# An attention and expert layer on one core: low-part subtractions and result sums all on VectorE, ScalarE's steps two slots behind

## The reference

```python
xn = layernorm(x)
s = attention(xn)          # layernorm, q = xn @ Wq (8 heads of 64), one shared k and v, l2-normed q and k,
                           # softmax(q k^T) v, @ Wout, layernorm
y = experts(xn)            # top 2 of 8 experts with a capacity, gelu MLP 256 -> 1024 -> 256, gated sum
return x + s * silu(y)
```

## Time and profile before

| | |
|---|---|
| median of 3 runs | 3028.18 us (3024.03 to 3028.85) |
| profiled execution | 3029.31 us, its span 3027.6 us |
| TensorE busy | 2777.8 us, 92% |
| VectorE busy | 2012.2 us, 66% |
| ScalarE busy | 1910.8 us, 63% |
| GpSimd busy | 1125.2 us, 37% |
| mean granted TensorE clock | 0.974 of full speed |
| low parts on VectorE, L1194 | 817 instructions, 1347 ns mean |
| low parts on GpSimd, L1313 | 215 instructions, 2049 ns mean |
| sums of the result on GpSimd, L1306 | 64 instructions, 1263 ns mean |
| exponentials, L843 | 1032 instructions, 1015 ns mean |

### The profile page before, as it was taken

How to read it: one execution, slowest core, us unless ns; L and a number is a source line. 1 busy time by engine, 2 the same in 40 slices (tenths; PEclk the granted TensorE clock), 3 DMA queues, 4 the chain that set the end, 5 groups by cost and what they waited for, 6 DMA issues and landing times.

```text
span 3027.6 us, 86214 instructions
## 1 busy us (share of the span) xinstructions
PE 2777.8 (92%) x38213; PEld 1847.3 (61%) x38277; DVE 2012.2 (66%) x2798; ACT 1910.8 (63%) x2435; POOL 1125.2 (37%) x707
## 2 busy tenths in 40 slices
PE   4999999988999989999999999999888889888896
PEld 3566666655666657666666666655555555555564
DVE  5777787789888733333333343378788888888775
ACT  6777767756766655565656565466666666666664
POOL 2444444414787400000000000055566656566454
PEclk8999999999999989999999999999999999999997
DMA  2213222003332011221121221101111111111101
GB/s 98 93 66 109 89 76 92 28 32 99 126 120 85 6 55 50 79 72 65 63 86 59 68 74 51 38 24 32 49 47 42 49 42 40 42 43 44 30 23 45
DMA packets 111013, 184.12 MB, mean 61 GB/s; under 512 B 12648, under 2 KB 78128, under 8 KB 110640
## 3 DMA queue, kind: packets, MB, share of 16 engines
q1 hardware_dynamic: 98352, 145.04, 14.6%
q0 software_dynamic: 12288, 33.57, 3.5%
HBM read 92.58 MB, written 85.98 MB: 59 GB/s over the span
## 4 chain that ended last, share of the span: by engine, by line
PE 64%; DVE 17%; ACT 9%; issue 7%; POOL 2%; DMA 1%; SPq 0%; ACTq 0%; DVEq 0%; POOLq 0%
PE pair L607 15%; PE bank L687 14%; PE pair L673 14%; DVE arena L1194 9%; ACT arena L843 6%; PE bank L637 5%; PE bank L628 4%; PE bank L626 4%; PE bank L588 2%; PE bank L546 2%; DVE o_rest L1129 1%; PE bank L657 1%; DVE q_n L1115 1%; POOL routed_rows L1271 1%; PE bank L576 1%
## 5 line engine op out<-in xcount | busy, mean ns | idle before, releaser
L1194 DVE TENSOR_TENSOR arena<-arena 128x1024 bf16<-128x1024 f32 (+1 forms) x817 | 1091.9, 1347 | 351.6 <-ACT arena L843 349.0
L843 ACT ACTIVATE arena<-pair 128x1024 f32<-128x1024 f32 (+1 forms) x1032 | 1017.2, 1015 | 319.4 <-PE pair L607 309.7
L607 PE MATMUL pair<-qT,kT 128*128 128x512 f16 (+1 forms) x4096 | 903.0, 388 | 136.7 <-ACT arena L843 133.6
L626 PE MATMUL bank<-vhl,arena 128*128 128x65 bf16 x8192 | 654.4, 194 | 4.0 <-DVE att L1187 4.0
L1313 POOL TENSOR_TENSOR arena<-arena 128x1024 bf16<-128x1024 f32 (+1 forms) x215 | 440.6, 2049 | 578.6 <-ACT arena L843 561.3
L628 PE MATMUL bank<-vhl,arena 128*128 128x64 bf16 x8192 | 655.0, 195 | 0.0
L626 PEld LDWEIGHTS bank<-vhl,arena 128*128 128x128 bf16 x8192 | 573.6, 100 | 56.3 <-DVE att L1187 4.4
L628 PEld LDWEIGHTS bank<-vhl,arena 128*128 128x128 bf16 x8192 | 555.3, 98 | 52.3 <-issue 1.9
L607 PEld LDWEIGHTS pair<-qT,kT 128*128 128x128 f16 (+1 forms) x4096 | 205.5, 96 | 598.8 <-issue 405.0
L1243 POOL TENSOR_TENSOR q_small<-q_small,minus_half 128x8 f32<-128x8 f32 x64 | 142.8, 2231 | 1015.8 <-DVE q_small L1111 1014.8
L637 PE MATMUL bank<-vhl,arena 128*128 128x65 bf16 x8192 | 421.2, 194 | 22.9 <-DVE arena L1194 17.1
(11 more groups left out here) (191 smaller groups left out, 2448.6 us busy)
## 6 DMA issues: line engine op xcount, KB each, us to landing
routed_rows<-h_f SPq DMA_DIRECT2D x80, 256.0 KB, 4.5
att<-routed_rows SPq DMA_DIRECT2D x40, 512.0 KB, 4.3
expert_rows<-att SPq DMA_DIRECT2D x40, 512.0 KB, 2.9
raw<-in_L_ffn_w SPq DMA_DIRECT2D x32, 512.0 KB
xn_rows<-s_hl SPq DMA_DIRECT2D x16, 512.0 KB, 2.9
xT_out<-xn_rows SPq DMA_DIRECT2D x64, 128.0 KB
w_lo<-in_L_attn_x SPq DMA_DIRECT2D x64, 128.0 KB
out<-w_lo SPq DMA_DIRECT2D x64, 128.0 KB, 2.0
```

The costliest lines, as they stand in the source:

```text
L607: t = nc.tensor.matmul(into, kT[g // BG % 2][rows, part, keys], qT[g % 2][rows, h, :], start=(turn == 0), stop=(turn == 1))
L626: nc.tensor.matmul(bank[:, at:at + DH + 1], p_top[:, s, cols, 1], V[:, kb, 0:DH + 1], start=(kb == 0 and qb == 0), stop=False, skip_group_ ...
L843: nc.scalar.activation(p_f32[:, n % NP, columns(n)], pairs[n % 2][:, columns(n)], ACT.Exp).then_inc(exped, 1)
L1194: nc.vector.tensor_tensor(p_lo[:, n % NP, c], p_f32[:, n % NP, c], p_top[:, n % NP, c, 1], ALU.subtract).then_inc(lowed, 1)
```

## The change

The set `on_pool` and its semaphore go: VectorE makes the low part of every step. The sum with x in `combine` is made on VectorE, right behind the product, instead of on GpSimd. ScalarE's cast of q and VectorE's low part of q stand one and two slots later (7 and 9) for all but the first four tiles; in `combine` f_both moves to slot 10, the tanh to 12, silu, product and sum to 14, the store to 16. No amount of work changes.

```diff
-    on_pool = [n % 4 == 3 and not R_AT <= place["scores", n] < SCATTER_AT + 2 * NT for n in range(NSTEP)]
-    pool_to = np.cumsum(on_pool).tolist()
...
-                pe.wait_ge(lowed, n + 1 - pool_to[n])
-                pe.wait_ge(lowed_pool, pool_to[n])
+                pe.wait_ge(lowed, n + 1)
...
-                yield from clock.at(Q_AT[t_id] + 6)
+                yield from clock.at(Q_AT[t_id] + (6 if t_id < GT else 7))
                 act.wait_ge(q_scaled, t_id + 1)
...
-                yield from clock.at(C_AT[t_id] + 10)
+                yield from clock.at(C_AT[t_id] + 12)
                 act.wait_ge(f_both, i + 1)
...
-                yield from clock.at(Q_AT[t_id] + 7)
+                yield from clock.at(Q_AT[t_id] + (7 if t_id < GT else 9))
                 dve.wait_ge(q_hi, t_id + 1)
...
-                yield from clock.at(C_AT[t_id] + 9)
+                yield from clock.at(C_AT[t_id] + 10)
                 dve.wait_ge(f_first, i + 1)
...
-                yield from clock.at(C_AT[t_id] + 12)
+                yield from clock.at(C_AT[t_id] + 14)
                 dve.wait_ge(c_tanh, i + 1)
...
+                dve.wait_ge(c_times, i + 1)
+                dve.wait_ge(x_again_loaded[i % 2], 16 * (i // 2 + 1))
+                dve.wait_ge(out_stored[i % 2], 16 * (i // 2))
+                nc.vector.tensor_tensor(res[i % 2], w, x_again[i % 2], ALU.add).then_inc(c_added, 1)
...
-                    if a is not None and not on_pool[a]:
+                    if a is not None:
                         low(a)
...
-                yield from clock.at(C_AT[t_id] + 14)
-                pool.wait_ge(c_times, i + 1)
-                pool.wait_ge(x_again_loaded[i % 2], 16 * (i // 2 + 1))
-                pool.wait_ge(out_stored[i % 2], 16 * (i // 2))
-                nc.gpsimd.tensor_tensor(res[i % 2], c_work[i % 2][:, D:2 * D], x_again[i % 2],
-                                        ALU.add).then_inc(c_added, 1)
...
-                yield from clock.at(C_AT[t_id] + 15)
+                yield from clock.at(C_AT[t_id] + 16)
                 sp.wait_ge(c_added, i + 1)
```

More of the change, by code:

```diff
@@ L361, in build_program @@
                              "q_hi", "q_lo", "q_turned", "qT_copied")]
-        scored, exped, lowed, lowed_pool, weighed = [sem(n) for n in (
-            "scored", "exped", "lowed", "lowed_pool", "weighed")]
+        scored, exped, lowed, weighed = [sem(n) for n in ("scored", "exped", "lowed", "weighed")]
         head_inv, divided = sem("head_inv"), sem("divided")
@@ L1301, in combine @@
                         bass.IndirectOffsetOnAxis(gather_from[k][:, t_id:t_id + 1], 0)).then_inc(y_gathered[i % 2], 16)
-                yield from clock.at(C_AT[t_id] + 14)
-                pool.wait_ge(c_times, i + 1)
-                pool.wait_ge(x_again_loaded[i % 2], 16 * (i // 2 + 1))
-                pool.wait_ge(out_stored[i % 2], 16 * (i // 2))
-                nc.gpsimd.tensor_tensor(res[i % 2], c_work[i % 2][:, D:2 * D], x_again[i % 2],
-                                        ALU.add).then_inc(c_added, 1)
[L1309 to L1314, removed]
             def main(kind, a, b):
-                if kind == "att" and a is not None and on_pool[a]:
-                    low(a)
+                pass
             clock.run(slots, main, [constants()] + [statistics(g) for g in reversed(range(NG))] + [route()] + [
```

## The result

The changed kernel takes 2898.13 us (2895.26 to 2902.57), the kernel before beside it 3028.51 us; the ratio is 0.9574, interval 0.9557 to 0.9590. The forecast was 2952 us, so the saving was 130 us and not 76. The sign and the range held; the time itself is that of the rival "TensorE-bound", 2897 us.

The account below looks back on a forecast made before the run. VectorE's stretched, late results were taken to hold up ScalarE and, through it, TensorE. Savings of 55 us late, 15 early, 5 from 600:800 and 1 at the end sum to 76: 3028 - 76 = 2952 us, range 2888 to 3008.

Parts of the forecast that it names:

- TensorE-bound: Rival: queueing goes entirely, late part runs at the pitch of 800:950; 97 late, 26 early, 8 elsewhere: 2897 us, chance 0.23.
- The cause of the waits: Late attention: GpSimd's subtraction stretches VectorE's instructions, so ScalarE waits 138 us at tanh and cast, TensorE 80 for exponentials.
- VectorE's total: VectorE late: 760 - 141 stretching + 131 subtractions + 29 sums = 779 us, 1.69 a step; early 1.70.
- How full VectorE can run: Attention: VectorE filled to 88.7%, as in 600:800, giving pitch 1.91, taken as 1.90 late (55 us saved).
- TensorE's own time: Late attention: the low clock costs up to 0.05 us a step, of which 0.01 was taken as regained.
- The distances: Tanh and q cast one slot further behind VectorE's results: three quarters of ScalarE's 138 us late waits go.
- tight place: q low part at slot 9, turn at 11: 0.6 us left, 0.6 needed; cost 0 to 30 us.
- The early part: Attention in 100:600: pitch from 1.95 to 1.89 us over 257 steps, saving 15 us.
- The sum: Result's sum with x moved to VectorE: 57 x 0.5 = +29 us late; shortens the end by 1 us.
- The slower rival: VectorE cannot be filled: share stays 81.7%, pitch 2.07 late, 2.08 early, together 3084 us; slower cases' chance 0.10.
- The case that it doesn't do what it says: Rival: stretching comes from gathers and powers, which stay; late load 2.06 us a step, rather over 3100; chance 0.03.

Follow-up runs that it names:

- The useless subtraction: Changed kernel plus a 128x944 subtraction on GpSimd, which nobody waits for, at each step whose subtraction it used to make: 3148.71 us, ratio 1.0395.
- the later turn: Changed kernel with TensorE's turn of q and ScalarE's copy two slots later (13 instead of 11): 2877.86 us, ratio 0.9514, beside the changed kernel.
- extra work put on it: Kernel with q's turn at 13 plus one useless 128x256 VectorE subtraction behind every second low part after the expert stage: 2920.65 us, ratio 0.9646.
- q's old slots: Changed kernel with q's cast and low part back at slots 6 and 7, the rest as changed: 2923.39 us, ratio 0.9574.
- the distances alone: Kernel before with only the slots changed; GpSimd keeps every fourth subtraction and the sum (slot 16, store 17): 3070.68 us, ratio 1.0068.
- the fills: Changed kernel plus two write-only fills of a 128x944 tile on GpSimd at the steps whose subtraction it used to make: 2903.40 us, ratio 0.9593.

## Why the prediction was right and where it wasn't

*The cause of the waits.* Right. GpSimd's subtraction holds VectorE's instructions up. The useless subtraction shows it without any dependence: 1420 ns where the changed kernel has 1220, and 247 us of time. Moving it alone brings 109 us. The kernel before shows it one by one: of its late 128x1024 subtractions the 141 with no GpSimd instruction beside them took 1218 ns in the mean and none over 1226; the 81 whose longest overlap was with GpSimd's 128x1024 subtraction took 1814 ns in the mean and up to 4023.

*VectorE's total.* Right in kind, a little high: 1.69 us a step forecast late, 1.65 measured; 1.70 early, 1.62 measured (424.8/262). Over the same 515 late steps VectorE was busy 827.0 us before and 830.4 after: the added subtractions and sums cost what the stretching had. The stretching went whole, to 1221 ns, and it was more than was counted: late the step of L1168 with s_xin (32 at 709 ns, now 484) is missing from the sum, early the groups said to be left out (11 low parts of the normalised rows fell from 1837 to 1222 ns, 11 small steps for `shift` from 922 to 153). The sum with x measured 0.43 us, where 0.5 was taken with its wait. The 1.14 us for each added subtraction was about right: the records give 534.7 us of union for 448, 1.19 each, and over the late steps 1.10 each of that overlaps with no record of another VectorE line.

*How full VectorE can run.* This is the step that failed. I took the 88.7% of 600:800 as the most it can hold, and from it a late pitch of 1.90; measured are 1.79, and a late saving of 117 us by steps, not 55. The fullest stretch of a trace is no limit. Of the 22.6 us in which VectorE stood idle in 600:800, nearly all were waits for the exponential; it was waiting, not full:

```profile
DVE arena L1194 <- ACT arena L843: 21.1, 18, 2.9
```

The changed kernel held 92.6% at 1.79 us a step, the later turn 94.5% at 1.74, and with extra work put on it VectorE reached 97.6%. With 1.65 us of work a step it was never the bound. The share isn't the whole of the miss: with 1.65 in place of 1.69 the prediction's own sum gives a pitch of 1.85 and a late saving of 78 us, so some 23 us of the miss lie in VectorE's total. What the old kernel had at 81.7% was not a full engine but single stretched instructions of 2 us and more in a chain that had one slot of slack.

*TensorE's own time.* Too small as well: I gave it 0.01 us a step, some 5 us, for a clock that recovers. Over the same 515 late steps TensorE stood still for 108 us before and 25 after, and its busy time fell too, from 912.5 to 878.9 us, so 34 of the 117 us are its own work getting shorter. The granted clock was at its lower level for 54.6 us of these steps before and for 10.2 after. TensorE's busy time for one matmul record was 100 ns there before (507 records) and 127 after (74), against 58.4 and 57.1 at the upper level, from which I estimate some 16 us for the clock. What shortened the records at the upper level isn't shown.

*The distances.* Mixed. The result chain's was worth 23 us (old and new slots on one chip), once the stretching was gone. The q steps' was worth nothing, as the prediction feared at its "tight place": I had taken 0 to 30 us for the turn, and the trace has 17.3 late, 15.7 early, 7.6 and 3.1 between, 44 in all, of which the later turn gets 23 back. In the changed kernel the low part that began at 2104.04 ended at 2104.73 and the turn began at 2104.87, after 0.82 us of standing:

```profile
2104.04 0.69 DVE L1115 TENSOR_TENSOR qhl<-q_n,qhl 128x512 f16<-128x512 f32 x1
```

```profile
2104.87 0.61 PE L554 MATMUL bank<-ident,qhl 128*128 128x128 f16 x8 [0.82 <-DVE qhl L1115]
```

*The early part.* Forecast 15 us, measured 7 over steps 20 to 283. TensorE's wait for the exponential fell from 28.1 to 9.8 us and the turn took most of it back; with the turn at 13, or with q's old slots, the same steps took 497 to 498 us, which is 12 to 13 less than before.

*The sum.* I gave it 29 us of VectorE late and 1 us at the end. It makes no difference where it is made: what GpSimd's version stretches is about what VectorE's costs. The tail took 41.8 us before and 41.9 after, and 40.0 in the repeat of the changed kernel, so a gain of 1 us can't be told from these traces.

*The rivals.* "TensorE-bound" is the one whose time came true, in part by luck. Its mechanism is the right one: the queueing goes, and its argument against, bursts at 93% of VectorE, was the wrong half. But its 131 us were 97 late, 26 early and 8 elsewhere, and measured are 117, 7 and some 6. Late it did not count on TensorE's own time falling below that of 800:950, and early it had nothing for the turn of q. The slower rival asked for a VectorE share below 83.7%, and it was 92.6. The case that it doesn't do what it says is out with L1193 at 1221 ns.

What stays open: the distances alone made the kernel slower by 0.7%, and the trace names the turn of q and the low parts, but outside the scatter stretch that trace is no longer than the kernel before's, and no run had only the result chain's distance on the kernel before. Nor was it found why the scatter stretch differed between chips.

## What to carry to other kernels

Before giving GpSimd a share of VectorE's work, measure the VectorE instructions that run beside it, by form, against a stretch where GpSimd is quiet: here one quarter of the subtractions on GpSimd cost VectorE about as much time as making them itself, and did it in pieces of up to 2.8 us (one subtraction of 4.02 us in place of 1.22) that a queue in order passes on to ScalarE and TensorE. A distance of slots in a hand-written order is worth what its two ends leave: when a step moves back, move its reader as well. And a share of busy time below 90% in some other stretch is no ceiling; the work per step against that of the bound engine says more.

## What the runs showed of the hardware

What GpSimd's instruction does with SBUF matters, and not only that it runs. Its 128x944 subtraction of 2.08 us beside VectorE's steps with two SBUF inputs stretched the mean from 1220 to 1420 ns; two fills of 0.89 us each at the same places, which only write, stretched nothing (1219 ns). The two differ in operation and length too, so reading as the cause is not isolated by them alone. The Trainium skill, "SBUF — State Buffer", section "SBUF: two separate sides", restricts the lock on such VectorE steps to GpSimd operations that read SBUF; both runs agree with it.

Not every GpSimd instruction that reads holds VectorE for the length of its record, though GpSimd's records are rough. In the changed kernel a power of 2.58 us ran from 2119.06, and two subtractions that began at 2118.88 took 2.37 us, as they do alone (2.35); of the 53 late subtractions beside such a power none took over 1226 ns. So a hold for the whole instruction, as the prediction names it, doesn't fit these small powers:

```profile
2119.06 2.58 POOL L1242 TENSOR_TENSOR q_small<-q_small,minus_half 128x8 f32<-128x8 f32 x1 [6.70 <-DVE q_small L1106]
```

```profile
2118.88 2.37 DVE L1193 TENSOR_TENSOR arena<-arena 128x1024 bf16<-128x1024 f32 x2
```

Whether VectorE holds GpSimd too is open. The gather instructions of GpSimd took 1274 ns in the mean in 2000:2930 before, 1615 in the changed kernel's 2000:2800 and 2026 where VectorE was 97.6% full. But beside the fills, with VectorE at 92.5% as in the changed kernel, they took 1365, so VectorE's share alone doesn't set it, and no run isolated the cause. It cost little here: in the changed kernel ScalarE waited once for gathered rows, 2.2 us.
